# Gated activations turned by VectorE through memory, down products two blocks behind, weights issued by ScalarE

## What is computed

```python
x = x + attention(layernorm(x), ...)
xt = layernorm(x)                                   # 4096 tokens x 512
scores = sigmoid(xt @ gate_w.T)                     # 8 experts
top_scores, top_idx = top_k(scores, 2)              # normalised, times 2.5
y_e = (silu(xt @ w1[e]) * (xt @ w3[e])) @ w2[e]     # hidden width 352
routed = sum over the 2 chosen e of top_score * y_e
shared = (silu(xt @ sw1) * (xt @ sw3)) @ sw2
out = x + routed + shared
```

## Time and profile before

| | |
|---|---|
| median of three runs | 1528.33 us (1523.52 to 1529.8) |
| the profiled execution | 1535.9 us, its span 1534.0 us |
| granted TensorE clock, mean | 0.965 |
| TensorE busy | 1414.4 us (92%) |
| VectorE busy | 893.3 us (58%) |
| ScalarE busy | 508.8 us (33%) |
| GpSimd busy | 452.3 us (29%) |
| bytes moved | 136.81 MB, mean 89 GB/s |

### The profile page before, as it was taken

The page is one execution under the profiler, slowest core; times in us unless marked ns, Lnnn a source line. Parts: engine busy times, 40 slices in busy tenths (PEclk is TensorE's granted clock), DMA queues, the critical chain, the costliest instruction groups (busy, mean ns, idle before and its releaser), DMA issues.

```text
span 1534.0 us, 21932 instructions
## 1 busy us (share of the span) xinstructions
PE 1414.4 (92%) x6059; PEld 704.4 (46%) x6060; DVE 893.3 (58%) x2655; ACT 508.8 (33%) x1042; POOL 452.3 (29%) x431
## 2 busy tenths in 40 slices
PE   6997999999999998899899984699999999999996
PEld 3552223333433332455455542355555555555553
DVE  4898998888788861678687864233333333333331
ACT  4662456766676677212021121011111111111110
POOL 0000000000000000000222252667777777777771
PEclk9996999999999999899899997799999999999998
DMA  7685310310320000466676752244444444444442
GB/s 219 217 237 156 80 39 4 78 43 5 68 58 4 5 5 16 135 195 180 158 174 176 180 101 50 48 67 71 69 69 69 69 69 69 69 70 70 69 69 35
DMA packets 124854, 136.81 MB, mean 89 GB/s; under 512 B 37046, under 2 KB 86590, under 8 KB 124774
## 3 DMA queue, kind: packets, MB, share of 16 engines
q1 hardware_dynamic: 101350, 96.56, 24.4%
q0 software_dynamic: 21520, 37.84, 14.4%
q10 hardware_dynamic: 1904, 1.46, 0.3%
HBM read 87.03 MB, written 48.83 MB: 89 GB/s over the span
## 4 chain that ended last, share of the span: by engine, by line
PE 72%; DVE 13%; DMA 5%; issue 5%; ACT 2%; SPq 1%; POOL 1%; ACTq 0%; DVEq 0%; POOLq 0%
PE psum L1046 28%; PE psum L1057 14%; PE psum L959 8%; PE psum L941 7%; PE psum L923 6%; PE psum L873 3%; DVE arena L1239 3%; DVE psum L1237 2%; PE psum L1029 2%; DMA xq<-xn_rows 2%; DMA xn_rows<-xg 2%; DMA attn_cur<-attn_rows 1%; PE psum L1020 1%; PE psum L944 1%; ACT arena L709 1%
## 5 line engine op out<-in xcount | busy, mean ns | idle before, releaser
L1046 PE MATMUL psum<-arena,xg_t 128*128 (+2 forms) x1648 | 520.1, 470 | 20.5 <-DVE xg_t L1209 19.9
L1046 PEld LDWEIGHTS psum<-arena,xg_t 128*128 128x128 f32 x1648 | 312.4, 195 | 182.8 <-issue 32.9
L781 ACT ACTIVATE arena<-psum 128x512 f32<-128x512 f32 (+3 forms) x640 | 303.6, 535 | 176.2 <-PE psum L941 87.3
L643 POOL DMA_INDIRECT table<-const,slot_i x64 | 62.5, 976 | 865.2 <-DVE slot_i L1424 756.1
L659 POOL DMA_INDIRECT xq<-xn_rows,quad_rows x284 | 272.2, 958 | 96.4 <-issue 88.9
L1057 PE MATMUL psum<-arena,act_t 128*128 (+3 forms) x618 | 282.5, 593 | 1.2 <-ACT act_t L809 0.7
L1239 DVE TENSOR_REDUCE arena<-psum 128x1 f32<-128x512 f32 x384 | 251.0, 685 | 30.5 <-PE psum L923 29.9
L923 PE MATMUL psum<-arena 96*128 96x512 bf16 (+3 forms) x640 | 219.1, 363 | 17.8 <-DVE arena L1237 9.6
L1320 DVE TENSOR_TENSOR act_sb<-psum,silu 128x352 f32<-128x352 f32 x103 | 54.0, 524 | 284.8 <-ACT silu L831 226.9
L941 PE MATMUL psum<-arena 99*128 99x512 bf16 (+3 forms) x640 | 215.0, 353 | 3.5 <-ACT arena L781 2.7
L831 ACT ACTIVATE silu<-psum 128x352 f32<-128x352 f32 x103 | 47.8, 464 | 466.8 <-PE psum L1046 410.5
(11 more groups left out here) (138 smaller groups left out, 894.6 us busy)
## 6 DMA issues: line engine op xcount, KB each, us to landing
arena<-qk_parts SPq DMA_DIRECT2D x48, 256.0 KB, 6.2
arena<-in_w SPq DMA_DIRECT2D x16, 704.0 KB
arena<-in_x SPq DMA_DIRECT2D x32, 256.0 KB, 4.4
x<-in_x SPq DMA_DIRECT2D x32, 256.0 KB
xn_rows<-xg SPq DMA_DIRECT2D x32, 256.0 KB
xq<-xn_rows SPq DMA_DIRECT2D x128, 64.0 KB
out_rows<-y_sb SPq DMA_DIRECT2D x32, 256.0 KB
qk_parts<-arena SPq DMA_DIRECT2D x16, 384.0 KB, 3.2
```

Source lines behind the costliest of these rows:

```text
L781: nc.scalar.activation(probs[:, at_b % PS, d * P:], psum[:, NA + at_b % NBK, 0:CH - d * P], ACT.Exp, scale=float(HD) ** -0.5).then_inc(s_e, 1)
L1046: i = nc.tensor.matmul(psum[:, bank + k % 2, 0:w], xg_t[:, k % 2, c, :], rhs, start=c == 0, stop=c == DC - 1)
```

## The change

The weights of the experts are issued by ScalarE instead of SyncE, in 24 parts (three per expert) over the first 28 steps of the shared stage. The three transposes `at` on TensorE and `at_copy` on ScalarE go. In their place `gated` writes its product in 32-column pieces, reordered, in two instructions; ScalarE stores the tile to memory (128 x 384), waits until it has landed, and loads it back in four quarters, of 384-byte pieces; VectorE turns it in one instruction (`turn_gated`). The down product and y are two tiles behind `up` instead of one, also in the routed stage, where the scatter goes from n - 2 to n - 3. The down products of the last three shared tiles are held until after the last `up`, two banks in turn, and the ranks of group 4 go from ahead of `up(31)` to behind it. The ring of turned activations has three places in the shared stage and two in the routed one. x is loaded four tiles ahead instead of five. A constant of 568 columns is replaced by one of 71 that is broadcast.

```diff
-COUNT_AT = {12: 0, 20: 1, 27: 2, 29: 3, 31: 4}
+COUNT_AT = {12: 0, 20: 1, 27: 2, 29: 3}
+HELD = 3
+W_STEPS = 28
@@ SyncE, shared(n, k)
-                load_expert(n // 4, n % 4)
                 if k < NT - 2:
                     load_quarters(n + 2, k + 2)
-                if k >= 1:
-                    store_y(sh, io["out"], n - 1, k - 1)
-                if k < NT - (XR - 1):
-                    load_row(n + XR - 1, k + XR - 1)
+                if k >= 2:
+                    store_y(sh, io["out"], n - 2, k - 2)
+                if 1 <= k < NT - (XR - 2):
+                    load_row(n + XR - 2, k + XR - 2)
@@ GpSimd, routed
-                if n >= 2:
-                    scatter(n - 2)
+                if n >= 3:
+                    scatter(n - 3)
@@ ScalarE
+                def turn_gated(n, k):
+
+                    act.wait_ge(ss["a"], n + 1)
+                    act.dma_start(act_rows[k % 2], act_sb[:, k % 2, :]).then_inc(ss[f"gated_stored_{k % 2}"], 16)
+                    act.wait_ge(ss[f"gated_stored_{k % 2}"], used(n, k) + 16)
+                    w = HP // QP
+                    for i in range(QP):
+                        act.dma_start(aq[i * QW:(i + 1) * QW, k % 2],
+                                      act_rows[k % 2][:, i * w:(i + 1) * w].rearrange("(g a) d -> a g d", g=QP)
+                                      ).then_inc(ss[f"gated_loaded_{k % 2}"], 16)
...
                 def step(n, k):
                     if ss is sh and k < count - 3:
                         to_copy(n + 3, k + 3)
-                    if k >= 1:
-                        at_copy(n - 1, k - 1)
                     if ss is sh:
+                        for i in range(3 * E * n // W_STEPS, min(3 * E, 3 * E * (n + 1) // W_STEPS)):
+                            load_expert(i // 3, i % 3)
...
                     nc.scalar.activation(silu[:, :], psum[:, 1 + k % 2, 0:H], ACT.Silu).then_inc(ss["silu"], 1)
+                    turn_gated(n, k)
@@ TensorE
-                    if k >= 1:
-                        at(n - 1, k - 1)
                     up(n, k, expert(n))
-                    if k >= 1:
-                        down(n - 1, k - 1, expert(n - 1))
+                    if k >= 2 and not (shared and n - 2 >= NT - HELD):
+                        down(n - 2, k - 2, expert(n - 2))
...
+                    ranks(len(GROUPS) - 2, NT)
+                    down(NT - 3, NT - 3, None)
+                    down(NT - 2, NT - 2, None)
+                    ranks(len(GROUPS) - 1, NT)
+                    down(NT - 1, NT - 1, None)
@@ VectorE
-                    nc.vector.tensor_tensor(act_sb[:, k % 2, 0:H], psum[:, 3 + k % 2, 0:H], silu[:, :], ALU.mult).then_inc(ss["a"], 1)
+                    nc.vector.tensor_tensor(place[:, 0:HC - 1], by_chunk(psum[:, 3 + k % 2, 0:whole], HC - 1),
+                                            by_chunk(silu[:, 0:whole], HC - 1), ALU.mult)
+                    nc.vector.tensor_tensor(place[:, HC - 1, 0:HL // QW], psum[:, 3 + k % 2, whole:H].rearrange("p (i b) -> p i b", b=QW),
+                                            silu[:, whole:H].rearrange("p (i b) -> p i b", b=QW), ALU.mult).then_inc(ss["a"], 1)
...
+                def turn_gated(n, k):
+                    dve.wait_ge(ss[f"gated_loaded_{k % 2}"], QP * (used(n, k) + 16))
...
+                    nc.vector.transpose(act_t[:, k % ring].rearrange("p c (g a) -> p g c a", g=QP),
+                                        aq[:, k % 2].rearrange("p g (c b) -> p g c b", c=HC)).then_inc(ss["ate"], 1)
...
                     if k >= 1:
-                        y(n - 1, k - 1)
+                        turn_gated(n - 1, k - 1)
+                    if k >= 2 and not (shared and n - 2 >= NT - HELD):
+                        y(n - 2, k - 2)
...
                     choose(len(GROUPS) - 1, 2)
                     slots(len(GROUPS) - 1)
+                    y(NT - 3, NT - 3)
+                    turn_gated(NT - 1, NT - 1)
                     block_list()
+                    y(NT - 2, NT - 2)
```

85 lines of the change are left out of this document (45 added, 40 removed).

## The result

The changed kernel took 1595.34 us (median of 4, 1588.44 to 1598.57) beside 1529.07 us for the kernel before (median of 4, 1523.52 to 1532.72): ratio 1.0448, 95% interval 1.0425 to 1.0472. It is slower by 66 us where 1498 us was forecast. On four further chips the same program, or one that differs only in idle instructions or in a loop written out, took 1548 to 1555 us beside 1522 to 1528: about 1.6% slower. So there are two losses to explain, one that stays (25 us) and one that only the first measurement shows (some 40 us net).

What follows compares the result with a forecast made beforehand. TensorE was taken to bound the routed stage fully and the shared stage apart from 37 us of stalls. Terms summed to -30.7 us, 1535.9 to 1505.2 profiled; less 7.6 for the median, 1498 us, range 1472 to 1538.

Steps and rivals of the forecast that it cites:

- Transposes leave TensorE: Both stages: 0.33 us less per block; routed period 7.65 to 7.32, -22.1 us over 67 periods; shared -9.9.
- limit of 4.1 us: Routed stage: store landing up to which ScalarE's loop stays under 7.32 us per block; 2.5 us assumed.
- second rival: Routed stage: the store's landing becomes the loop, slower than before; at 5.0 us landing +64, 1562 us; chance 0.13.
- Ramp, -8.5: Start of routed stage: up(1) directly follows up(0), up(3) starts at 988.9 instead of 997.4; -8.5 us.
- Shared loop, stalls of 40 us for 37: Shared stage: 245.5 us of work plus 40 of stalls, 285.5 for 295; -9.5 us.
- the 3.6 of the ranks: End of shared loop: up(31) no longer waits behind the ranks of group 4; -3.6 us.
- the bounds of 15 to 75: Shared-stage stalls: 15 us if only waits for VectorE and counts stay, 75 if DMA-bound at 9.5 us a step.
- the relief of SyncE's queue: Shared stage: 704 KB weight parts leave SyncE's queue ahead of quarter loads; taken as nearly cancelling 28% more bytes.
- First rival, DMA-bound: Shared stage: step of 9.5 us instead of 8.33, +31, total 1529 us; chance 0.19.
- VectorE's added work, covered: Shared stage: about 0.65 us more per step, just covered in plain steps; 20 us in full without cover.
- Held products and seam, +8: Between stages: last sigmoid 4.5 us later, down(30) about +2, pairs read +1.5; together +8 us.
- End, +5: After the last routed up: the bare trip puts the last scatter 14.3 us behind it instead of 9.3; +5 us.

Runs made afterwards that it cites:

- the kernel before, shifted: Kernel before with 290 always-fulfilled waits (145 instructions) put between ScalarE's shared and routed stages: 1526.41 us beside 1524.24.
- the run with such bytes: Kernel before plus, per shared step, an unused 192 KB store and four loads in 384-byte pieces, landings awaited a step later; 71-column constant: 1532.67 us.

## Why the prediction was wrong, step by step

*Transposes leave TensorE, 7.32 us per block: right.* 7.31 between undisturbed ups, and 513.7 to 514.6 us for the routed stage in every kernel of the study that has the trip there, the first measurement apart. The landing stays under its limit of 4.1 us: 3.59 in the block shown, 1.94 (1301.47 to 1303.41) on another chip, where 2.5 was taken. The second rival, which places the landing in the routed stage's period, did not happen there.

*Ramp, -8.5: half right.* up(1) follows up(0) at once, as said. But 4 to 5.5 us of the gap in the earlier trace rows was one of the stands of the first measurement, not the structure of the kernel before. From up(0) to up(1) it needed 9.8 us when shifted (1.3 of them the moved table load), not 13.9, and 8.3 to 8.6 in the three other kernels with the same stage. The whole routed stage took 543.9 and 540.7 to 541.0. The change is worth 27 to 30 us there, not 30.6 by the forecast or 34 by the first trace. The row said "remote" in the open, and I took its time as a price that the change removes.

*Stands of ScalarE, not in the prediction.* 563.2 - 514.0 = 49 us in the first measurement. Not shown: their cause. Shown: the program does not bring them by itself, since it ran without any on two other chips, and they are no instruction fetches by the count of packets. They lift the loss from the 1.6% that the change costs elsewhere to 4.5%.

*Shared loop, stalls of 40 us for 37: the step that failed.* The sum was 245.5 us of work and, less the 3.6 of the ranks, 36.4 of stalls; the loop took 322.1, so 77 us of stalls, 88 by the mean of seven (334), both outside the bounds of 15 to 75. The work was right, 8.33 us in a plain step that nothing holds up. I held the bytes against the relief of SyncE's queue and let them cancel. The runs show this in its place:

- A second queue did not relieve the first one; its landing waits got longer. SyncE's wait for the normalised rows is 70.5 us in the kernel before, shifted (61.3 in the first trace), and 113.5 with the weights alone on ScalarE, on the same chip.
- Weights and bytes, each alone, add 9 to 10 us to the loop, all of it behind up(11), where experts are chosen and the table is written.
- ScalarE's wait for its own store behind its own weights is the greatest piece. Its next attention copy, weight issue and silu are queued behind it. Taking either away, the weights (309.3) or the wait (307.9), gives back 25 or 26 us of 334; in the plain steps the two together are all of the loss.

I had named these three as queued behind the wait, and wrote that the landing decides from 4.1 us, but priced it for the routed stage alone. In the shared stage landings of 10 us are in the trace. The second rival was the right mechanism in the wrong stage.

*First rival, DMA-bound: not as put.* The DMA share was to be 0.80 or more; it was 0.66, at 188 GB/s, so 285 GB/s at full share where the sum took 252. Mean throughput was not the limit; the time of single landings was. The Trainium skill's rule on pieces under 512 B (DMA: Bandwidth & Descriptors, Specifications) can be weighed only as a bound: the run with such bytes lost nothing in the plain steps and 9 us in the whole loop, all causes together, ScalarE's waits a step later among them; pieces of 512 B or more were not tried.

*VectorE's added work, covered: right.* 0.57 us per step alone cost 1 us, which is within the spread of single profiles; the 0.15 us of the second gated instruction was not in that run.

*Held products and seam, +8: right* within 2 us: 41.7 for 43.6, and 43.3 to 45.0 elsewhere. The sigmoid came 4.3 us later, 4.5 was taken.

*End, +5: right.* 26.2 for 19.4, elsewhere 24.9 to 27.0 for 18.9 to 19.6.

*The sum on other chips*, loop and seam 378 for 329 (+48), routed -27 to -30, end +5, start +1: 24 to 27, as timed (1548.6 - 1522.5 = 26). The loop misses by 53 us (40 longer, with 12.5 us less work in it). The prices found part by part are not to be added up to it: those of the weights and of the wait depend on each other, and the later turn brings a ring of its own. What the change gives in the routed stage is taken back in the shared one, where the same trip meets weights, attention tiles, normalised rows and table writes. Without that part the kernel is 1.7% faster than before, of which 21 to 25 us of 28 are the change's. Open: how much of the loss behind up(11) belongs to the table writes.

## What to carry to other kernels

Taking a transpose off the bounding engine by a trip through memory paid here in the stage in which the DMA queues are quiet and not in the one in which bulk loads run: judge it stage by stage, by the longest landing seen in that stage, and try it in each alone. An engine with other work should not wait for a transfer that it has just issued behind its own bulk loads: take the loads out of its queue, or place the wait a step later, and then look for the ring that the later place closes. A price found by adding one part alone says little of parts that wait for each other; try them in pairs, and read plain steps apart from busy ones. Check a wait without a known releaser on a second chip before it goes into a sum.

## What the runs showed of the hardware

- One program took 1588 to 1599 us in the first measurement and 1545 to 1554 us on two other chips, while the medians of the kernel before differ by 0.4% (1529.07, 1522.52 and 1522.99). Its routed stage was 563.2 us against 513.9 and 514.0, with ScalarE standing mostly 4 to 8 us, 21 times, before an activation whose input was long done; its shared loop was shorter, 322.1 against 337.3 and 329.7. Instruction packets in the routed stage were eight with and without the stands.
- Moving 704 KB loads from a busy queue to a second one did not shorten the first queue's landings: on one chip its waits for a 256 KB store went from 70.5 us (30 times) to 113.5 us (30 times). With the added trip they were 144.1 us in the first measurement, where they had been 61.3.
- A 192 KB store landed in 1.9 us in the routed stage (DMA share 0.61), and in 1.9 to 10.0 us in the shared one (0.66) of the same run. The 10.0 came with a 704 KB load 2.9 us ahead of it in its queue and small table writes beside it; with no weights at all the median was 1.9 before the table writes began and 4.4 after.
- TensorE's granted clock was 0.50 (1.2 of 2.4 GHz) at the end of a wait of 5.46 us and 0.75 in the mean over the 6.6 us after it, in which the 16 products of an up took 6.60 us for 4.96.
